# Cross-attention with image tokens: the one-off setup in another order, with column tiles, other overlays, and part of its DMAs issued from ScalarE's queue

## What is computed

```python
q = split_heads(x @ w_q)                       # 20 heads of 32
k, v = split_heads(text @ w_k), split_heads(text @ w_v)
out_text = softmax(q k^T / sqrt(32)) v
k_ip, v_ip = split_heads(ip @ w_k_ip), split_heads(ip @ w_v_ip)
out_ip = softmax(q k_ip^T / sqrt(32) + mask_ip) v_ip   # mask: 0 or -10000, from boxes on a grid
out = (out_text + out_ip) @ w_out + b_out + x
```

## Time and profile before

| | us |
|---|---|
| median of 3 runs | 745.49 (742.37 to 745.92) |
| profiled execution | 749.81 |
| its span | 748.0 |
| TensorE busy in the span | 703.8 (94%) |
| first maxima transposed for block 1 | 119.70 |
| block 1, block 2 | 38.8, 38.9 |

### The profile page before, as it was taken

One profiled execution on the slowest core, in us unless ns is written; L12 is line 12 of the kernel. 1 busy time (PEld: TensorE's weight loads), 2 busy tenths in 40 slices (PEclk: granted clock), 3 DMA queues, 4 the chain that ended last, 5 costly groups with the idle time before them and its releaser, 6 DMA issues.

```text
span 748.0 us, 18848 instructions
## 1 busy us (share of the span) xinstructions
PE 703.8 (94%) x6384; PEld 638.1 (85%) x6384; DVE 538.0 (72%) x1694; ACT 286.1 (38%) x615; POOL 205.5 (27%) x347
## 2 busy tenths in 40 slices
PE   4959797999999999999999999999999999999987
PEld 3847356899999999999999998989898989999876
DVE  3232157878787878878887878797979797878764
ACT  1011022616161626253534444352626261717051
POOL 1000042423233232414150505051414242323223
PEclk9978999999999999999999999999999999999979
DMA  9989923334352525253434444444443443434310
GB/s 247 289 189 264 208 44 99 84 103 130 87 152 73 160 67 159 78 147 89 135 91 132 100 129 102 127 102 133 96 140 90 118 111 96 133 91 113 88 48 36
DMA packets 85120, 91.34 MB, mean 122 GB/s; under 512 B 10768, under 2 KB 69776, under 8 KB 85068
## 3 DMA queue, kind: packets, MB, share of 16 engines
q1 hardware_dynamic: 85084, 90.87, 46.2%
HBM read 40.42 MB, written 10.62 MB: 68 GB/s over the span
## 4 chain that ended last, share of the span: by engine, by line
PE 74%; DMA 9%; DVE 7%; SPq 6%; issue 2%; ACT 1%; POOL 0%; DVEq 0%; ACTq 0%
PE psum L930 31%; PE psum L1022 9%; PE psum L978 7%; PE psum L1010 6%; PE psum L1005 5%; DMA q_stack<-aux_a 5%; PE psum L1030 3%; SPq L430 3%; PE psum L881 2%; PE psum L1031 2%; PE psum L842 2%; SPq L454 2%; PE psum L891 2%; PE psum L1045 2%; DMA q_stack<-mask_scratch 1%
## 5 line engine op out<-in xcount | busy, mean ns | idle before, releaser
L747 DVE TENSOR_REDUCE neg_max<-psum 128x2 f32<-128x292 f32 x320 | 145.1, 454 | 67.9 <-PE psum L978 67.5
L502 POOL TENSOR_TENSOR attn<-o_parts 128x128 f32<-128x128 f32 x160 | 73.0, 456 | 419.9 <-DVE o_parts L785 419.9
L930 PE MATMUL psum<-wo_both,at_hi 128*128 128x320 f32 x640 | 153.3, 312 | 0.0
L978 PE MATMUL psum<-k_stack,q_stack 104*128 104x154 f32 x640 | 111.8, 285 | 8.7 <-DMA q_stack<-mask_scratch 4.7
L930 PE MATMUL psum<-xt_hi,wq_hi 128*128 128x256 f32 x400 | 115.2, 288 | 1.4 <-DVE xt_lo L717 1.4
L930 PE MATMUL psum<-xt_hi,wq_lo 128*128 128x256 f32 x400 | 112.5, 281 | 0.0
L930 PE MATMUL psum<-xt_lo,wq_hi 128*128 128x256 f32 x400 | 112.4, 281 | 0.0
L772 DVE TENSOR_TENSOR p_lo<-psum,p_hi 128x512 f16<-128x512 f32 x160 | 107.9, 683 | 2.9 <-ACT psum L600 2.6
L930 PEld LDWEIGHTS psum<-wo_both,at_hi 128*128 128x128 f32 x640 | 109.5, 188 | 0.0
L598 ACT ACTIVATE p_hi<-psum 128x512 f16<-128x512 f32 x160 | 95.2, 595 | 29.5 <-PE psum L1005 29.3
L978 PEld LDWEIGHTS psum<-k_stack,q_stack 104*128 104x128 f32 x640 | 89.6, 192 | 16.6 <-DVE neg_max L748 11.0
(11 more groups left out here) (87 smaller groups left out, 1274.9 us busy)
## 6 DMA issues: line engine op xcount, KB each, us to landing
q_stack<-q_hi SPq DMA_DIRECT2D x128, 96.0 KB
x_in<-in_x SPq DMA_DIRECT2D x16, 640.0 KB, 4.1
x_res<-in_x SPq DMA_DIRECT2D x16, 640.0 KB, 5.0
out<-out_sb SPq DMA_DIRECT2D x32, 320.0 KB
q_stack<-q_hi SPq DMA_DIRECT2D x128, 64.0 KB
q_stack<-q_lo SPq DMA_DIRECT2D x64, 96.0 KB
q_stack<-q_lo SPq DMA_DIRECT2D x64, 64.0 KB
q_stack<-aux_a SPq DMA_DIRECT2D x48, 64.0 KB, 2.4
```

What stands on the lines that cost most here:

```text
L502: nc.gpsimd.tensor_tensor(cols, o_parts[:, qt, 0:4, :], o_parts[:, qt, 4:8, :], ALU.add).then_inc(att_half, 1)
L747: nc.vector.tensor_reduce(dst[:, :, 0], src[:, :, 0:TEXT], AX_X, ALU.max, negate=True)
L930: last = nc.tensor.matmul(ps, l(c), r(c), start=(i == 0), stop=(i == len(terms) - 1))
L978: last = nc.tensor.matmul(scores[sc % 2][:, i * CTX:(i + 1) * CTX], q_stack[0:ROW_MAX, h, P * qt:P * (qt + 1)], k_stack[batch][0:ROW_MAX, ...
```

## The change

- SyncE's queue: the context by batch, five key weights, x; then, after the transposes of the context, all image key weights in one DMA and w_q; the value weights as before. The image value weights come in block 0 behind the first query stack and ahead of x for block 1. w_o comes at the end of block 0.
- ScalarE's queue: identity, the small inputs and constants at the start; the two halves of the mask (the first after group 2); the twelve key DMAs of batch 1, ahead of ScalarE's value copies in block 0; at the end of block 0 the sixteen tail-value DMAs, a wait for their landing, and the bias.
- Image keys: 16 context rows are stationary, and four heads-of-four go to four column tiles (output partitions 0, 32, 64, 96) with 160 columns each; ScalarE copies the rows out and five small matmuls with a picking matrix (`key_pick`) turn them. Image values in the same way; the rest values (36 rows) in two column tiles of 320 columns.
- Values: units in the order batch 0, rest, batch 1, image, at other places of block 0, some of them in parts.
- w_q is split in five column pieces, each due for its query group; w_o in five pieces within block 1, by ScalarE and VectorE.
- GpSimd writes the key tails' zeros at the start, the constant rows of `k_stack` and the ones of `v_tail` (in place of DMAs), and copies the key tails (in place of VectorE).
- Other tensors share addresses: the setup's now lie over others of the loop, and k high and low have room of their own.

The diff, cut to its core:

```diff
+SP_FIRST = [(FRONT, "STK", 0), (NEXT, "XIN"), (FRONT, "STK", 1)]
...
-V_UNITS = [(keys, c0, c1) for keys in ("ip", "rest", "batch 0", "batch 1") for c0, c1 in ((0, 512), (512, D))]
-V_PLACES = {("S", 0, 0, 0): (0, 1), ("S", 1, 0, 0): (2, 3), ("S", 2, 0, 0): (4, 5), None: (6, 7)}
-W_O_PLACE = ("S", 2, 0, 0)
+V_UNITS = [("batch 0", 0, 512), ("batch 0", 512, D), ("rest", 0, D), ("batch 1", 0, 512), ("batch 1", 512, D), ("ip", 0, D)]
+V_SPLIT_TURN = {0: 0, 1: 1, 3: 2, 4: 3}
+V_PLACES = {
+    ("S", 0, 0, 0): ((0, 0, 8), (1, 0, 8)), ("S", 0, 1, 0): ((2, 0, 4),), ("S", 1, 0, 0): ((2, 4, 8),),
+    ("S", 1, 0, 1): ((3, 0, 3),), ("S", 1, 1, 0): ((3, 3, 6),), ("S", 1, 1, 1): ((3, 6, 8),),
+    ("S", 2, 0, 0): ((4, 0, 8),), ("S", 2, 1, 0): ((5, 0, 8),),
+}
+W_O_PLACES = {("ST", 2, 0): 0, ("ST", 2, 1): 1, ("ST", 3, 0): 2, ("ST", 3, 1): 3, ("ST", 4, 0): 4}
...
+        def keys_to_stack(queue, b):
+            for row, part in K_PARTS:
+                for j in range(4):
+                    queue.dma_start(k_stack[b][row:row + DH, j:HEADS:4, :].bitcast(F32),
+                                    part[DH * j:DH * (j + 1), :, b, :].bitcast(F32)).then_inc(s_kst[b], 16)
...
+                sp.dma_start(ctx_main[:, b, :], ctx[b, 0:P, :]).then_inc(s_ctx[b], 16)
+                sp.dma_start(w_kv[:, :, P * g:P * (g + 1)], column_group(wk, g)).then_inc(s_wk[g], 16)
+            sp.dma_start(x_in[:], x_rows[0:QB, :].rearrange("(a p) d -> p a d", p=P)).then_inc(x_loaded, 16)
+            sp.wait_ge(s_ctx_tr, 2 * BATCHES + 1)
+            sp.dma_start(w_k_ip[:], wk_ip.rearrange("(c p) n -> p c n", p=P)).then_inc(s_wk_ip, 16)
...
+                    sp.wait_ge(s_klo, GROUPS + 1)
+                    sp.wait_ge(stored, 16 * BATCHES)
+                    keys_to_stack(sp, 0)
+                for stage, kind, args, gen, sc in it.steps(SP_STEPS if it.back else SP_FIRST):
...
+                        if not it.back:
+                            sp.dma_start(w_v_ip, wv_ip.rearrange("(c p) n -> p c n", p=P)).then_inc(s_wv_ip, 16)
...
+                    sp.wait_ge(s_vp, len(V_UNITS))
+                    sp.dma_start(wo_raw[:, KC:2 * KC, :], wo.rearrange("(c p) n -> p c n", p=P)).then_inc(s_wo, 16)
...
+            nc.gpsimd.memset(k_ip_rows[:], 0.0).then_inc(s_ip_zero, 1)
+            for b in range(BATCHES):
+                nc.gpsimd.memset(k_tail[b][:].bitcast(mybir.dt.uint32), 0).then_inc(s_ktail_zero, 1)
+            pool.wait_ge(s_row_raw, 16)
+            pool.wait_ge(s_ktail_zero, BATCHES)
+            for b in range(BATCHES):
+                rows = slice(ROW_MASK, STACK)
+                nc.gpsimd.tensor_copy(k_stack[b][rows, :, :].rearrange("p (g j) k -> p g (j k)", j=4),
+                                      row_raw[rows, :].unsqueeze(1).to_broadcast([STACK - ROW_MASK, GROUPS, 4 * CTX])
+                                      ).then_inc(s_rows, 1)
+            pool.wait_ge(s_rows, BATCHES)
+            pool.wait_ge(s_ones, 16)
+            for b in range(BATCHES):
+                groups = slice(1 - b, GROUPS)
+                nc.gpsimd.tensor_copy(v_tail[b][:, groups, :], v_tail[0][:, 0, :].unsqueeze(1).to_broadcast(
+                    [P, GROUPS - 1 + b, 8 * VW])).then_inc(s_ones_all, 1)
             for b in range(BATCHES):
                 pool.wait_ge(s_kst[b], 16 * 12)
-            for b in range(BATCHES):
-                nc.gpsimd.memset(k_tail[b][:].bitcast(mybir.dt.uint32), 0).then_inc(s_ktail_zero, 1)
-            pool.wait_ge(s_wsplit_hi, 2)
-            nc.gpsimd.tensor_tensor(wo_lo, wo_raw[:, KC:2 * KC, :], wo_hi.bitcast(F32), ALU.subtract).then_inc(s_wsplit, 1)
+                for j in range(4):
+                    nc.gpsimd.tensor_copy(k_tail[b][0:STACK, j:HEADS:4, 32 * j:32 * j + TAIL],
+                                          k_stack[b][0:STACK, j:HEADS:4, P:CTX].bitcast(F32)).then_inc(s_ktail, 1)
...
+            act.dma_start(ident[:], c_ident).then_inc(s_ident, 16)
+            for b in range(BATCHES):
...
+            act.dma_start(row_raw[ROW_MASK:STACK, :], c_rows).then_inc(s_row_raw, 16)
+            act.dma_start(v_tail[0][:, 0, :], c_ones).then_inc(s_ones, 16)
+                if g in (2, 4):
+                    b = 0 if g == 2 else 1
+                    act.wait_ge(s_mval, 4 * (b + 1))
+                    act.dma_start(mask_dram[:, b * SEQ:(b + 1) * SEQ], mask[:]).then_inc(stored, 16)
+            act.wait_ge(s_ip_zero, 1)
+            act.wait_ge(s_kp, K_IP + 1)
+            for j in range(4):
+                rows = slice(32 * j, 32 * j + BATCHES * IP)
+                nc.scalar.activation(k_ip_rows[rows, :, j, :], k_bank(K_IP)[rows, 0:GROUPS * DH].rearrange("p (g d) -> p g d", d=DH),
+                                     ACT.Copy).then_inc(s_ip_rows, 1)
+            act.wait_ge(s_kp, K_IP_T + 1)
+            for b in range(BATCHES):
+                nc.scalar.activation(k_hi[:, :, b, TEXT:CTX],
...
+            def fill_tails(b):
+                act.wait_ge(s_vc, len(V_UNITS))
+                for j in range(4):
+                    r = 32 * j
+                    rows = 64 * (j // 2) + REM * b
+                    act.dma_start(v_tail[b][r:r + REM, :, VW * j:VW * j + DH], v_rest[rows:rows + REM, :, j % 2, :]
+                                  ).then_inc(s_vt[b], 16)
+                    act.dma_start(v_tail[b][r + REM:r + TAIL, :, VW * (4 + j):VW * (4 + j) + DH],
+                                  v_rest_ip[r + IP * b:r + IP * (b + 1), :, :]).then_inc(s_vt[b], 16)
+            def w_high(n):
+                if n < GROUPS:
+                    cols = slice(P * n, P * (n + 1))
                     act.wait_ge(s_wq, 16)
-                    nc.scalar.activation(wq_hi[:], wq_raw[:], ACT.Copy).then_inc(s_wsplit_hi, 1)
+                    nc.scalar.activation(wq_hi[:, :, cols], wq_raw[:, :, cols], ACT.Copy).then_inc(s_wsplit_hi, 1)
+                else:
+                    c = n - GROUPS
+                    act.wait_ge(s_wo, 16)
+                    nc.scalar.activation(wo_hi[:, c, :], wo_raw[:, KC + c, :], ACT.Copy).then_inc(s_wsplit_hi, 1)
...
+            for n in range(GROUPS):
+                w_high(n)
+                if n < NX:
+                    x_high(n, n + 1, general[n])
...
+                        if (kind, *args) == ("S", 0, 0, 0):
+                            act.wait_ge(s_klo, GROUPS + 1)
+                            act.wait_ge(stored, 16 * BATCHES)
+                            act.wait_ge(s_rows, BATCHES)
+                            keys_to_stack(act, 1)
+                    if isinstance(t, int) and t == 1 and (kind, *args) in W_O_PLACES:
+                        w_high(GROUPS + W_O_PLACES[(kind, *args)])
...
+                    fill_tails(0)
+                    fill_tails(1)
+                    act.wait_ge(s_vp, len(V_UNITS))
+                    act.wait_ge(s_vt[0], 16 * 8)
+                    act.wait_ge(s_vt[1], 16 * 8)
+                    act.dma_start(bias[:], b_out.rearrange("(a n) -> a n", a=1).to_broadcast([P, D])).then_inc(s_bias, 16)
...
+            nc.vector.tensor_copy(rest_t[:], rest).then_inc(s_ctx_t, 1)
...
+            def w_low(n):
+                dve.wait_ge(s_wsplit_hi, n + 1)
+                if n < GROUPS:
+                    cols = slice(P * n, P * (n + 1))
+                    nc.vector.tensor_tensor(wq_lo[:, :, cols], wq_raw[:, :, cols], wq_hi[:, :, cols].bitcast(F32), ALU.subtract
                                             ).then_inc(s_wsplit, 1)
+                else:
+                    c = n - GROUPS
+                    nc.vector.tensor_tensor(wo_lo[:, c, :], wo_raw[:, KC + c, :], wo_hi[:, c, :].bitcast(F32), ALU.subtract
...
+            pe.wait_ge(s_wk_ip, 16)
+            pe.wait_ge(s_klo, 3)
+            heads = w_k_ip[:].rearrange("p c (g j d) -> p c g j d", j=4, d=DH)
+            for c in range(CC):
+                for j in range(4):
+                    last = nc.tensor.matmul(k_bank(K_IP)[32 * j:32 * j + BATCHES * IP, 0:GROUPS * DH],
+                                            rest_t[:, c, BATCHES * REM:], heads[:, c, :, j, :],
+                                            start=(c == 0), stop=(c == CC - 1))
+            last.then_inc(s_kp, 1)
...
+            pe.wait_ge(s_ip_rows, 4)
+            for g in range(GROUPS):
+                n = BATCHES * IP
+                last = nc.tensor.matmul(k_bank(K_IP_T)[:, n * g:n * (g + 1)], k_ip_rows[:, g, :, :].rearrange("p j d -> p (j d)"),
+                                        key_pick[:], start=True, stop=True)
+            last.then_inc(s_kp, 1)
...
+                    ps = v_bank(n)
+                    for c in range(first, end):
+                        begin, stop = c == 0, c == CC - 1
+                        if keys == "ip":
+                            heads = w_v_ip.rearrange("p c (g j d) -> p c g j d", j=4, d=DH)
+                            for j in range(4):
+                                last = nc.tensor.matmul(ps[32 * j:32 * j + BATCHES * IP, 0:GROUPS * DH],
```

(62 more changed lines are left out.)

253 lines of the change are left out of this document (99 added, 154 removed).

## The result

| | before | after |
|---|---|---|
| median, us | 746.91 (742.37 to 751.35, 19 runs) | 752.35 (747.29 to 756.19, 19 runs) |
| ratio to before | | 1.0079 [1.0058, 1.0100] |
| profiled execution, span | 749.81, 748.0 | 751.59, 749.8 |
| T (first maxima transposed for block 1) | 119.70 | 112.10 |
| block 1 (T to the next such transposes) | 42.45 | 54.42 |

The change made the kernel 0.8% slower; 738.5 was predicted. The trace has the whole mechanism, so the account goes by it: T came 7.6 us earlier, block 1 grew by 12.0, and 2.5 came back in block 2 and later (-7.6 + 12.0 - 2.5 = +1.9, the span's 1.8 but for rounding). A correction to the earlier trace rows: 119.7 to 158.5 is a steady period laid over the start of block 1, not the block.

A forecast was written before the change was run, and what follows sets the result against it. TensorE's matmuls fill 94% of the span, so setup counts only through T. T 13.9 us earlier and block 1 longer by 7.0 sum to -6.9: 742.9 profiled, 738.5 as median, range 724 to 750.

The forecast's parts named there:

- Start: Setup: context awaited by batch, identity not queued behind all of it; keys start at 10.3 instead of 14.52, gain 4.2.
- rival C: GpSimd's copies hold VectorE throughout, +6, or two issuers slow each other more than by turns: 744.5 us; chance 0.16.
- Text keys: Setup: five groups of 4.2 us and four sets of counts give 22.7; GpSimd's hold adds 2, ending at 35.0.
- Image keys: Setup: column tiles overlap only between neighbours, 4.4 us; with copies and small matmuls done at 41.6.
- Rival D: Column tiles run four at a time, 2.2 us less in each four-tile stretch: 734 us; chance 0.10.
- Mask: Setup: mask transfers taken as hidden, 1.5 us at worst, so TensorE's stop for the mask is gone.
- SyncE and x: Block 0: first scores at 68 instead of 83.06; x behind image value weights lands at 78.2, TensorE waits some 9 us.
- Rest of block 0: From x's landing at 78.2 to T: 27.6 us of scores, values and waits, giving T = 105.8, 13.9 earlier.
- Block 1, the tails: ScalarE's sixteen tail DMAs delay its first exponential to T + 14.8 from T + 8.1; 5.5 us taken, bounds 0 and 7.
- Block 1, w_o's parts: VectorE gets five low parts of w_o, 3.9 us of work, in block 1; cost taken as 1.5, bounds 0 to 4.
- Later blocks: After block 1: loop bodies and tail left alone, so no term; a steady block stays at 38.9 us.
- Rival A: Column tiles don't overlap, each of three tiled stretches costs 8.8 us and not 4.4: 752 us; chance 0.15.

The follow-up runs named there:

- e1: Changed kernel, with GpSimd waiting for VectorE's small mask operations before it copies the stack rows: 747.93 us, ratio to before 1.0021.
- e9: Changed kernel, with VectorE's five small mask operations behind its copies of the transposed context, GpSimd left as it was: 751.26 us, ratio to before 1.0062.
- e2: Changed kernel, with x for block 1 issued ahead of the image value weights instead of behind them: 741.0 us, ratio to before 0.9934.
- e7: Changed kernel with the edits of e1, e2, e6 and e9 together: 728.39 us, ratio to before 0.9770.
- e8: e7 with w_o read ahead of the tail transfers and its five splits earlier in block 1: 723.32 us, ratio to before 0.9703.
- e4: Changed kernel with all column-tiled matmuls writing to the first column tile, so some keys and values are wrong: 769.62 us, ratio to before 1.0333.
- e10: Changed kernel with the second batch's twelve key transfers on SyncE's queue again, behind block 0's second query stack: 747.49 us, ratio to before 1.0005.
- e5: Changed kernel without the sixteen tail-value transfers, those values left out of the attention: 746.12 us, ratio to before 0.9994.
- e6: Changed kernel with image values before batch 1's, tail transfers on SyncE's queue, w_o and bias behind block 1's first maxima copies: 743.77 us, ratio to before 0.9957.
- e11: e8 with e10's edit, the second batch's keys on SyncE's queue: 719.42 us, ratio to before 0.9640.

## Why the prediction was wrong, step by step

The prediction missed the measured median by 13.9 us and had the direction wrong. The 13.9 are 8.7 in the trace (+1.8 instead of -6.9), 3.7 because the two profiled executions lay on different sides of their medians, 1.4 because before's median rose with more runs. The 8.7 are +6.3 in T, +5.0 in block 1 and -2.5 later. Three steps failed: the start of the keys, the landing of x, and what the tails' issues hold up in block 1.

- *Start: failed, +8.1.* Forecast 10.3, measured 18.37. I took the constants for present and VectorE's copies for first. The hold by GpSimd, of which I took 2 us and put it at the counts, was 5.0, and stood ahead of the keys; the other 3.1 are the constants. That is rival C's mechanism, for nearly the whole of both copies, at another place. Shown by e1 and e9. The Trainium skill's "SBUF — State Buffer" (Who interferes with whom) has, beside the rule that I cited, that casts and tensor_scalar operations can take the shared port pair for a whole instruction; the rows at 11.03 and, in e9, at 11.24 agree. I had applied the page only to `inside`, which lost nothing here (2.27) and 0.5 in e2 (2.74).
- *Text keys: right, but for the first group.* From start to end 25.4 against 24.7, with no wait at the counts and a first group of 7.04. The same code in e7 and e8, with the same 0.61 us of idling ahead, took 6.91 and 4.20 there, with a granted clock of 1.00 over both. What decides between them stays open.
- *Image keys: right on the safe side.* Rival D held: 2.37 against my 4.4, and e4 shows what is saved, 6.5 us a time. My reading that only neighbours overlap was wrong.
- *Mask: right.* No stop is left; the queries started 6.7 late and took 10.7 against 9.5, so they ended 7.9 late.
- *SyncE and x: right in kind, short in size.* First scores at 76.79 and x at 89.22 are 8.8 and 11.0 late; 7.9 came from the queries. The step that failed is the landing of x, which I put together from durations measured in a queue alone: 13.3 after its issue, against 16.2. I had asked only whether two issuers slow each other's issues, not whether the second one's transfers slow the first one's. e10 shows both.
- *Rest of block 0: 22.9 against 27.6.* This gave back 4.7 of the 11.0. The rest and image values took 8.1 against 8.8, though the first of them ran at a granted clock of 0.50 to 0.65 (85 to 93; 3.39 against 2.35 for the same work at 1.00). Of before's waits in this stretch, 0.19, 1.63 and 1.93, only the last came again (1.86); GpSimd's product, which is gone, gave nothing there. The remainder wasn't taken apart.
- *Block 1, the tails: failed, 8.9 against 5.5.* I had counted only the exponentials behind ScalarE's sixteen issues. First behind them is its copy of the next queries, behind that VectorE's subtraction, behind that the maxima that free the score banks: TensorE stood from T + 6.5, before any exponential is due (T + 8.1 in the earlier trace rows), and on until ScalarE was free. e5 leaves the issues out and gets 8.6 back; e6 does them from another queue and gets 10.1, w_o's later place included.
- *Block 1, w_o's parts: 3.1 against 1.5.* VectorE did them in 0.81 to 1.11 us each, late in the block, where it is last. The 3.1 is what is left beside the 8.9; that the parts cost it is argued from e8, which takes 2.3 out of block 1 by their place and the read's, while block 2 grows by 1.4.
- *Later blocks:* nothing forecast, -2.5 came: 1.1 in block 2 (38.77 against 39.82), the rest in small pieces behind it. No run took this apart.

Rival A named the measured time, 752, for a reason that is wrong: the tiles do overlap, and without that the kernel is another 19 us slower by the times, 16 in the trace (e4). None of the rivals had the mechanism whole; C and D each had a part of it. What made the change slower than before is shown by what undoes it: the tails on ScalarE (e6, 9.1 us faster than after), x behind the weights (e2, 10.8), the second queue (e10, 5.5) and GpSimd's casts (e1, 4.3) add up to 29.7, and e11, which has them all with w_o's places and e9's order, is 32.8 faster. The sum of the four is uncertain by some 8 us, so the agreement is no finer than that. What the reordering and the tiles gained was hidden under these four.

## What to carry to other kernels

When work is moved to an engine that looks idle, follow the queue behind it for two more engines: what the moved issues hold is not what that engine does next but what others wait for from it. A transfer on a second queue may not run beside the first one's at no price; whatever is urgent goes first on one queue, and bulk goes behind it. And before small VectorE operations are given a start time, look at what GpSimd does in those microseconds.

## What the runs showed of the hardware that was not expected

- Four float column tiles of 160 columns each overlapped nearly fully: 64 records in 2.37 us, in 8.87 to one place.
- GpSimd's cast held an 8x32 VectorE operation with one input for 2.77 us, though it does 0.2 us of work.
- 1.18 MB of small rows on a second queue cost 640 KB on the first one 3.6 us of landing (16.2 against 12.6).
